# A transformer block with an eight-expert FFN on one core: the batch loop written out, and the hand-over copies replaced by buffers chosen by parity

## What is computed

```python
h = einsum('bhid,oi,od->bho', x, weighted_sum, weight)      # token mix, x is (8, 512, 256, 4)
h = h + attention(layernorm(h))   # 16 heads of 16, rotary, q and k normalised, softmax(q.k / 4), out projection
# FFN on x_flat = layernorm(h), 8 experts, hidden size 1024:
probs = sigmoid(x_flat @ Wg + bg)
weights = probs * (probs > 0.5)
hid = relu(einsum('td,edh->eth', x_flat, W1) + b1[:, None, :])
expert_out = einsum('eth,ehd->etd', hid, W2) + b2[:, None, :]
h = h + einsum('te,etd->td', weights, expert_out)
```

## Time and profile before

| what | value |
|---|---|
| median of 3 runs | 2021.08 us (2020.14 to 2027.73) |
| the profiled execution | 2029.17 us, its span 2027.4 us |
| PE matmul busy | 1911.6 us, 94% |
| ACT, DVE, POOL busy | 1142.6, 792.3, 678.6 us |
| DMA | 176.92 MB, mean 87 GB/s |
| granted clock of TensorE, mean | 0.974 |

### The profile page before, as it was taken

One profiled execution on the slowest core, in us unless ns is written; L12 is line 12 of the kernel. 1 busy time (PEld: TensorE's weight loads), 2 busy tenths in 40 slices (PEclk: granted clock), 3 DMA queues, 4 the chain that ended last, 5 costly groups with the idle time before them and its releaser, 6 DMA issues.

```text
span 2027.4 us, 36619 instructions
## 1 busy us (share of the span) xinstructions
PE 1911.6 (94%) x13152; PEld 1211.9 (60%) x13152; DVE 792.3 (39%) x1660; ACT 1142.6 (56%) x1969; POOL 678.6 (33%) x570
## 2 busy tenths in 40 slices
PE   5679888899999999999999999999999999999999
PEld 4246543577547764567646675467655776456666
DVE  6756933547203380145602472133810456013000
ACT  2644666544765457644765447654576446754444
POOL 1103422324323242333423343232423334233443
PEclk8779999999999999999999999999999999999999
DMA  4113332332112221131212312122221322113221
GB/s 154 38 53 113 105 130 84 123 138 84 63 64 105 97 83 63 66 130 67 84 63 87 113 66 81 63 105 95 72 75 63 109 91 84 63 63 103 104 96 53
DMA packets 40461, 176.92 MB, mean 87 GB/s; under 512 B 4056, under 2 KB 17120, under 8 KB 23904
## 3 DMA queue, kind: packets, MB, share of 16 engines
q1 hardware_dynamic: 40288, 174.52, 24.2%
HBM read 153.54 MB, written 20.97 MB: 86 GB/s over the span
## 4 chain that ended last, share of the span: by engine, by line
PE 77%; issue 7%; DVE 7%; ACT 2%; POOL 1%; ACTq 0%; DVEq 0%; POOLq 0%
PE bank_h L859 28%; PE bank_f L878 10%; PE bank_f L880 10%; PE bank_f L881 10%; PE bank_o L788 5%; PE bank_s L776 3%; PE bank_s L692 2%; PE bank_s L693 2%; PE bank_s L694 2%; DVE tmp_b L976 1%; PE bank_s L761 1%; POOL hl L549 1%; DVE y L899 1%; PE bank_s L842 1%; ACT hh L669 1%
## 5 line engine op out<-in xcount | busy, mean ns | idle before, releaser
L549 POOL TENSOR_TENSOR hl<-h,hh 128x512 f16<-128x512 f32 x512 | 608.4, 1189 | 1148.2 <-ACT hh L669 670.7
L859 PE MATMUL bank_h<-x,w1s 128*128 128x512 f16 x3072 | 756.0, 383 | 19.5 <-issue 9.1
L666 ACT ACTIVATE h<-bank_h,b1s 128x512 f32<-128x512 f32 x512 | 353.5, 690 | 468.6 <-PE bank_h L859 452.7
L878 PE MATMUL bank_f<-w2s,hh 128*128 128x256 f16 x2048 | 563.2, 275 | 2.1 <-DVE acc L1091 1.3
L880 PE MATMUL bank_f<-w2s,hh 128*128 128x256 f16 x2048 | 561.1, 274 | 0.0
L881 PE MATMUL bank_f<-w2s,hl 128*128 128x256 f16 x2048 | 560.9, 274 | 0.0
L859 PEld LDWEIGHTS bank_h<-x,w1s 128*128 128x128 f16 x3072 | 287.6, 99 | 345.7 <-issue 49.9
L669 ACT ACTIVATE hh<-bank_h,b1s 128x512 f16<-128x512 f32 x512 | 352.7, 689 | 0.0
L636 ACT ACTIVATE probs<-bank_s 128x512 f32<-128x512 f32 x480 | 262.3, 604 | 153.7 <-PE bank_s L776 153.6
L878 PEld LDWEIGHTS bank_f<-w2s,hh 128*128 128x128 f16 x2048 | 202.2, 99 | 113.8 <-issue 41.0
L1091 DVE SCALAR_TENSOR_TENSOR acc<-bank_f,gw,acc 128x256 f32<-128x256 f32 x256 | 106.1, 476 | 349.9 <-PE bank_f L881 349.8
(11 more groups left out here) (137 smaller groups left out, 1788.8 us busy)
## 6 DMA issues: line engine op xcount, KB each, us to landing
w1s<-w_parts SPq DMA_DIRECT2D x56, 1024.0 KB, 4.8
w2s<-w_parts SPq DMA_DIRECT2D x56, 1024.0 KB, 4.8
xraw<-in_x_t_dram SPq DMA_DIRECT2D x32, 512.0 KB, 4.1
raw<-in_w_dram SPq DMA_DIRECT2D x16, 1024.0 KB, 6.4
w_parts<-w1s SPq DMA_DIRECT2D x8, 1024.0 KB, 8.8
w_parts<-w2s SPq DMA_DIRECT2D x8, 1024.0 KB, 10.7
out_dram<-acc SPq DMA_DIRECT2D x16, 256.0 KB, 6.1
raw<-in_qkv_w_t_dram SPq DMA_DIRECT2D x1, 768.0 KB, 6.8
```

Of the source, the lines that this page charges most:

```text
L549: pool.tensor_tensor(hl[n % HBUFS][:], h32[n % 2][:], hh[n % HBUFS][:], ALU.subtract)\
L666: act.activation(h32[n % 2][:], bank_h[n % 2][:, :], ACT.Relu, bias=b1s[:, e, m:m + 1]).then_inc(h_hi.sem, 1)
L859: last = pe.matmul(bank_h[n % 2][:, :], w[:, wp, k, m * P:(m + 1) * P], x16[:, xp, k, :], start=(k == 0 and wp + xp == 0), stop=(k == DK - ...
L878: pe.matmul(o, high, w[:, 0, m, :], start=(m == 0 and t % 2 == 0), stop=False, skip_group_check=True)
```

## The change

The loop of the four compute engines and that of SP become Python loops, so all 8 batches stand in the program one after another and every wait is for a constant. `x16`, `gw` and `acc` exist twice, chosen by the batch's parity, in the place that the two sets of buffers had before (the memory used is the same). The attention of batch b writes straight into set b % 2 and the FFN reads it there. `hand_x` and `hand_acc` are gone with their three instructions per batch; the multiplication by `unscale` moves into `gates` and takes the place of the copy L1056. The waits change as follows:

- f1 of chunk 0 waits for `ln2_lo` in place of `handed_x`.
- ACT's first write to `x16` of batch ab waits until the f1 of batch ab-2 are all done, in place of `handed_x`.
- DVE's `project` of batch ab waits until batch ab-2 is stored (`stored`, `acc_done`), in place of `handed_acc`.
- `acc` waits for `accn_ready` in place of `handed_acc`.

The core of the diff:

```diff
-                if c == HM // 2:
-                    order.append(("hand_acc", 0))
...
-                if hand and c == CHUNKS:
-                    order.append(("hand_x", 0))
...
-               ("logits", TT - 1): [("hand_x", 0), ("f1", 0)],
+               ("logits", TT - 1): [("f1", 0)],
...
-        x16n = sb("x16n", [P, 2, DK, TOKENS], F16)
-        x16 = sb("x16", [P, 2, DK, TOKENS], F16)
-        gwn = sb("gwn", [P, TT, EXPERTS])
-        gw = sb("gw", [P, TT, EXPERTS])
-        accn = sb("accn", [P, TT, D])
-        acc = sb("acc", [P, TT, D])
+        x16s = [sb(f"x16_{i}", [P, 2, DK, TOKENS], F16) for i in range(2)]
+        gws = [sb(f"gw{i}", [P, TT, EXPERTS]) for i in range(2)]
+        accs = [sb(f"acc{i}", [P, TT, D]) for i in range(2)]
...
-            with eng.Fori(1, BATCHES - 1) as i:
+            for i in range(1, BATCHES - 1):
                 for stage, n in ordered(merged):
                     steps(stage, n, i, i + 1)
...
-            with sp.Fori(1, BATCHES - 2) as i:
+            for i in range(1, BATCHES - 2):
                 body(i, True, True)
...
-                    wait(act, handed_x, ab, 0)
-                    copy(x16n[:, 0, :, n * P:(n + 1) * P], tile_ps[n % 2]).then_inc(ln2_wide.sem, 1)
+                    wait(act, z_ready, ab - 1, 0)
+                    copy(x16s[ab % 2][:, 0, :, n * P:(n + 1) * P], tile_ps[n % 2]).then_inc(ln2_wide.sem, 1)
...
                     if n == 0:
-                        wait(pe, handed_x, fb, 1)
+                        wait(pe, ln2_lo, fb, TT)
...
-                    wait(dve, handed_acc, ab, 0)
+                    wait(dve, stored, ab - 1, 0)
+                    wait(dve, acc_done, ab - 1, 0)
+                    accn = accs[ab % 2]
                     ins = dve.tensor_tensor(accn[:, n, :], bank_s[n % 2][:, 0:D], resid[:, n, :], ALU.add)
...
-                    dve.tensor_copy(gwn[:], wg[:]).then_inc(accn_ready.sem, 1)
+                    if ab == 0:
+                        dve.tensor_copy(gws[0][:], wg[:]).then_inc(accn_ready.sem, 1)
+                    else:
+                        dve.tensor_tensor(gws[ab % 2][:], wg[:], unscale[:].unsqueeze(1).broadcast_to([P, TT, EXPERTS]),
+                                          ALU.mult).then_inc(accn_ready.sem, 1)
...
-                elif stage == "hand_x":
-
-                    if fb is not None:
-                        wait(dve, z_ready, fb, CHUNKS)
-                    wait(dve, ln2_lo, ab, TT)
-                    dve.tensor_copy(x16[:], x16n[:]).then_inc(handed_x.sem, 1)
-                elif stage == "hand_acc":
-
-                    wait(dve, stored, fb, 0)
-                    wait(dve, acc_done, fb, 0)
-                    wait(dve, accn_ready, fb, 2)
-                    if isinstance(fb, int) and fb == 0:
-                        dve.tensor_copy(gw[:], gwn[:]).then_inc(handed_acc.sem, 1)
-                    else:
-                        dve.tensor_tensor(gw[:], gwn[:], unscale[:].unsqueeze(1).broadcast_to([P, TT, EXPERTS]),
-                                          ALU.mult).then_inc(handed_acc.sem, 1)
-                    dve.tensor_copy(acc[:], accn[:]).then_inc(handed_acc.sem, 1)
```

More of the change, by code:

```diff
@@ L110, in bodies, with merge @@
         prep += [(start + at, *stage) for at, stage in zip(early if e == 2 else late, stages)]
-    def merge(waiting, hand, done=0):
+    def merge(waiting, done=0):
         waiting, order = sorted(waiting, key=lambda s: s[0]), []
@@ L145, in bodies @@
         first += [step[1:]] + between.get(step[1:], [])
-    return first, merge(attention + prep, True, done=2), merge(attention, True), merge([], False)
+    return first, merge(attention + prep, done=2), merge(attention), merge([])
 def exps_first(order):
@@ L367, in build @@
         accn_ready = signal("accn_ready", 2)
-        handed_x = signal("handed_x", 1)
-        handed_acc = signal("handed_acc", 2)
         z_ready = signal("z_ready", CHUNKS)
@@ L501, in store @@
                     wait(sp, acc_done, b, EXPERTS * TT - TT // 2 * (1 - half))
-                    sp.dma_start(out[b].rearrange("(t p) d -> p t d", p=P)[:, tiles], acc[:, tiles])\
+                    sp.dma_start(out[b].rearrange("(t p) d -> p t d", p=P)[:, tiles], accs[b % 2][:, tiles])\
                       .then_inc(stored.sem, 16)
@@ L848, in steps @@
                     if n == 0:
-                        wait(pe, handed_x, fb, 1)
-                    if m == 0 and isinstance(fb, int) and fb == 0:
+                        wait(pe, ln2_lo, fb, TT)
+                    if m == 0 and fb == 0:
                         pe.wait_ge(parts_lo, PIECES * e + PIECES // 2)
@@ L858, in steps @@
                         for wp, xp in ((0, 0), (0, 1), (1, 0)):
-                            last = pe.matmul(bank_h[n % 2][:, :], w[:, wp, k, m * P:(m + 1) * P], x16[:, xp, k, :],
+                            last = pe.matmul(bank_h[n % 2][:, :], w[:, wp, k, m * P:(m + 1) * P], x16s[fb % 2][:, xp, k, :],
                                              start=(k == 0 and wp + xp == 0), stop=(k == DK - 1 and wp == 1),
@@ L1034, in steps @@
                     for t in range(TT):
-                        dve.tensor_scalar(normed[:, t, :], accn[:, t, :], mean[:, t:t + 1], y1[:, t:t + 1],
+                        dve.tensor_scalar(normed[:, t, :], accs[ab % 2][:, t, :], mean[:, t:t + 1], y1[:, t:t + 1],
                                           ALU.subtract, ALU.mult).then_inc(ln2_out.sem, 1)
@@ L1039, in steps @@
                     cut = slice(n * P, (n + 1) * P)
-                    dve.tensor_tensor(x16n[:, 1, :, cut], wide[:, n % 2], x16n[:, 0, :, cut], ALU.subtract)\
+                    x16 = x16s[ab % 2]
+                    dve.tensor_tensor(x16[:, 1, :, cut], wide[:, n % 2], x16[:, 0, :, cut], ALU.subtract)\
                        .then_inc(ln2_lo.sem, 1)
@@ L1059, in steps @@
                     for s in range(2):
-                        cut = accn[:, 2 * s:2 * s + 2, :].rearrange("p t d -> p (t d)")
+                        cut = accs[ab % 2][:, 2 * s:2 * s + 2, :].rearrange("p t d -> p (t d)")
                         ins = dve.tensor_tensor(cut, bank_s[s][:, :], cut, ALU.add)
                     ins.then_inc(accn_ready.sem, 1)
-                elif stage == "hand_x":
-                    if fb is not None:
-                        wait(dve, z_ready, fb, CHUNKS)
-                    wait(dve, ln2_lo, ab, TT)
-                    dve.tensor_copy(x16[:], x16n[:]).then_inc(handed_x.sem, 1)
-                elif stage == "hand_acc":
-                    wait(dve, stored, fb, 0)
-                    wait(dve, acc_done, fb, 0)
-                    wait(dve, accn_ready, fb, 2)
-                    if isinstance(fb, int) and fb == 0:
-                        dve.tensor_copy(gw[:], gwn[:]).then_inc(handed_acc.sem, 1)
-                    else:
-                        dve.tensor_tensor(gw[:], gwn[:], unscale[:].unsqueeze(1).broadcast_to([P, TT, EXPERTS]),
-                                          ALU.mult).then_inc(handed_acc.sem, 1)
-                    dve.tensor_copy(acc[:], accn[:]).then_inc(handed_acc.sem, 1)
-                elif stage == "acc":
-                    wait(dve, handed_acc, fb, 2)
+                elif stage == "acc":
+                    acc, gw = accs[fb % 2], gws[fb % 2]
+                    wait(dve, accn_ready, fb, 2)
                     wait(dve, acc_done, fb, TT * n)
-                    if isinstance(fb, int) and fb == 0:
+                    if fb == 0:
                         scale_v.link(dve, dve.tensor_scalar(gw[:, :, n], gw[:, :, n], unscale[:, n:n + 1], None,
```

## The result

| | before | changed |
|---|---|---|
| median of 6 runs each | 2024.11 us (2020.14 to 2027.73) | 2010.36 us (2006.99 to 2015.23) |
| ratio, with 95% interval | | 0.9933 [0.9915, 0.9952] |
| profiled execution (span) | 2029.17 us (2027.4) | 2008.53 us (2006.6) |
| PE busy in its span | 94% | 95% |

The changed kernel is 0.67% faster, 13.75 us against before's six runs. The prediction said 2011.0 us, and the measured median is 0.6 us from it. It expected 10.0 us less, though, against a median of 2021.08 us from three runs; with six runs before's median is 2024.11. So the predicted time is right and the predicted difference 3.75 us too small.

What follows compares the result with a forecast made beforehand. PE was taken to bound the kernel, with a stall at each of five loop jumps. Jumps 9.6 us plus input copy 0.4 us made 10.0 us, so 2021.1 - 10.0 = 2011 us, range 2004 to 2017 us.

Steps and rivals of the forecast that it cites:

- What bounds the kernel: PE, busy 94% of 2027.4 us; time can only be won where PE stands still or runs slow.
- The loop written out: Five taken PE branches go at batch boundaries, each worth 237.55 - 235.63 = 1.92 us: 9.6 us, bounds 8.7 to 10.3.
- Constants for registers: Waits computed in the loop become constants: 0 us, since one piece took 21.70 and 21.66 us; 2 us kept for range.
- The input copy: L1068, exposed only before batch 0's first f1, where PE waited 0.43 us: worth 0.4 us, upper bound 0.69.
- The other copies: Sum and gate copies on DVE (L1075, L1077, L1079), 0.85 us per batch: taken as 0, upper bound batch 0's 0.85 us.
- the new waits: Waits on `project`, ACT's `x16` write and f1 of chunk 0 are met early enough: 0 us.
- The median: Whole kernel: median 2021.1 us less 10.0 us gives 2011 us, 0.5% less; forecast chance 0.80.
- The stall did not come back (1): Batch boundary: the 1.97 us stall belongs there or another wait replaces it, leaving 0.4 us gained, 2020.7 us; chance 0.07.
- straight code did not starve PE (2): Longer straight code makes PE's instruction fetches late twice per batch, adding 23 us: 2034 us; chance 0.03.
- The third, more than the jumps: DVE's 0.85 us in batch 0, registers' 2 us and less low clock at the start also count: 2006 us; chance 0.10.
- The rule against the change: At about 108 ns per compare-and-branch, PE's five jumps are worth an estimated 0.5 us; time would stay near 2020.

Runs made afterwards that it cites:

- experiment 2: Kernel before with its loops kept, only PE's loop given a prefetch hint for its closing branch: 2011.47 us, ratio 0.9944.
- experiment 3: Kernel before with only PE's loop written out; ACT, DVE, POOL and SP keep theirs, copies stay: 2013.74 us, ratio 0.9960.
- experiment 4: Kernel before with every loop written out except PE's, copies stay: 2021.86 us, ratio 1.0002.
- experiment 5: Changed kernel with a two-round loop, its body one wait long met, added on PE ahead of each of batches 1 to 6: 2011.32 us.
- experiment 1: Kernel before with all loops written out, the hand-over copies and their waits kept: 2011.21 us, ratio 0.9952.
- experiment 9: Kernel before run again unchanged, for its second profile: 2024.78 us.
- experiment 10: Kernel before with loops written out and copies kept, each hand-over copy doubled for three quarters of its data into a spare tile: 2009.58 us.
- experiment 7: The changed kernel run again unedited (the repeat): 2010.21 us, ratio 0.9936.

## Why the prediction was right, and where its size was off

- **What bounds the kernel** held: PE, with one visible stall at each of five boundaries.
- **The loop written out, 9.6 us: right in mechanism, the gain too small because of its base.** Experiments 2, 3, 4 and 5 show that the stall is PE's fetch at the far jump, that no other engine's loop takes part in it, and that nothing comes late behind it. The step that was off is the base behind "I take 1.92", the entry stretch of 235.63 us taken as what every stretch would become. The jump itself was sized rightly for that profile: all its stretches are of the longer length, so 5 x 1.92 = 9.6 us is what its five jumps cost. But the changed kernel's stretches are 235.00 to 235.25 us, and each of the six gave some 0.6 us more, 3.5 us in all, which the sum put at nothing. The two make the 13.1 us that went from these stretches. In the second profile of before the split is another: four of the five stretches behind a jump and the entry stretch are short, but the jumps cost more, 5 x (237.75 - 235.03) = 13.6 us, two clock drops included. At the boundary a jump took 1.95 to 2.02 us over the plain step of 0.11 in the first profile, 1.99 to 2.48 in the second, and 1.85 to 2.12 in experiment 4. One stretch was a thin base for a term of five.
- **Constants for registers, taken as 0.** On PE it is 0 within 0.06 us a batch (experiment 4's entry stretch). On ACT and DVE it was not looked at, and rows 7 could not show it: their piece lies from 219 us behind the bias matmul of batch 1 to 5 us behind the next, and the five places where PE waits 0.06 to 0.10 us longer lie 8.7 to 83.7 us behind one. The cost is 0.4 us a batch (experiment 3 against 1). In stretches of the shorter length it is won back, and kernels with registers reach 235.0 us as well (experiments 2 and 9); in those of the longer it is part of the 0.6 us. So its net effect in the six stretches is open between 0 and 2.5 us, where the range held 2 us. How much of the 3.5 us is the change's and how much the length that an execution of before happens to take is open with it.
- **The input copy, 0.4 us: right place, 0.58 us.** The 0.43 us was PE's idle time by the row, counted from the modelled end of the gates' last matmul. In the changed kernel f1 starts 0.16 us ahead of that end (133.71 against 132.15 + 1.72 = 133.87), so the distance to the last input part gives the price.
- **The other copies and the new waits at 0** held: for the copies by experiments 1 and 10, for the new waits by the changed kernel's stretches, which are within 0.07 us of experiment 1's on the mean and show no new wait of PE.
- **The median.** The forecast of 2011 us hit partly by luck, two errors in balance: a base 3 us too low (three runs of before) and a gain 3.75 us too small (2.7 us too small by experiment 7, whose runs of before have a median of 2022.92 us).
- **The rivals.** The stall did not come back (1), and straight code did not starve PE (2): in the changed kernel the instruction queue moved fewer packets, 105 against 120. The third, more than the jumps, lies nearer to the measured gain than the forecast (15 and 10 us, measured 13.75), but hardly by its causes: DVE's 0.85 us in batch 0 did not count, the clock of the start is noise, and of the registers up to 2.5 us is open.
- **The rule against the change**, about 108 ns for a compare-and-branch (the Trainium skill, Advanced Engine Details and Errata, section Control Flow Timing), did not hold for PE's taken branch, which took 3.4 us over the body and 0.21 to 0.23 us over three instructions. The rule on fetches, as cited in experiment 5, agrees with PE's branches.

## What to carry to other kernels

A hardware loop around a long body can cost its busiest engine a fetch at every jump: look at the branch records of each engine. Here PE, with the longest body, paid alone, and a prefetch hint on its branch gave as much as writing all loops out. Take the base of a saving from several stretches or a second profile, not from the one that looks clean. A copy on an engine with slack is free until the one place where the bound engine stands waiting for it.

## What the runs showed of the hardware

- A taken branch of PE over its whole loop body took 3.34 to 3.90 us (15 jumps in three profiles), of which 1.7 to 2.3 us were idle PE; over three instructions it took 0.21 to 0.23 us; with a prefetch hint 0.35 us.
- Behind two of these jumps, after PE had been busy at full clock and then idle for 2.32 and 2.16 us, the granted clock fell to the lower level (1.2 of 2.4 GHz) for 3.4 us, in which 8 matmul steps took 0.427 instead of 0.216 us each. So a far jump can cost its own length and a clock drop on top. It happened at 2 of 15 jumps; that the stall is the cause is read from the order of the two alone.
- One code had two lengths of a stretch, 235.0 and 235.63 us, with DVE busy 1.1 us more and POOL 0.5 us less in the longer (experiment 2).
- A short DVE instruction can be held up beside a long one of POOL. In the changed kernel a DVE instruction on 128x32 elements, which takes 0.19 us alone, took 1.08 us beside POOL's `hl` and ended with it:

```profile
139.32 1.15 POOL L540 TENSOR_TENSOR hl<-h,hh 128x512 f16<-128x512 f32 x1 [0.34 <-ACT hh L660]
139.44 1.08 DVE L1047 SCALAR_TENSOR_TENSOR wg<-lg,pg 128x32 f32<-128x32 f32 x1
```

In the repeat it slipped in just ahead of POOL:

```profile
139.77 0.19 DVE L1047 SCALAR_TENSOR_TENSOR wg<-lg,pg 128x32 f32<-128x32 f32 x1
139.89 1.15 POOL L540 TENSOR_TENSOR hl<-h,hh 128x512 f16<-128x512 f32 x1 [0.58 <-ACT hh L660]
```

PE waits for this result in batch 0: from its first f1 to the first bias matmul it is 8.56 us in the first and 7.25 us in the repeat. Of the 1.3 us, 0.9 are this wait; the other 0.4 stand in four matmuls (L827) that took 1.02 instead of 0.60 us, with the granted clock at its lower level from 140.2 us on in the first, just ahead of them, and from 141.0 us on in the repeat, behind them. In all twelve profiles this distance has one of two lengths, 8.5 us (five profiles) or 7.3 us (seven), and DVE's instruction took 1.0 to 1.1 us in the former and 0.19 us in the latter. That such meetings of DVE and POOL also make the two lengths of the stretches fits the busy times, but no run changed it alone, so it stays open.
